# Gate and up products of the shared expert made inside the attention, their clamp made by GpSimd on the way back

## The reference

```
x = x + cross_attention(layernorm(x), ctx)      # 16 heads of 32; q, k, v and the softmax are fake-quantized
h = layernorm(x)
scores = sqrt(softplus(h @ router.T))           # 32 experts
top 4 of scores + expert_bias, their scores normalized to sum 1
x = x + sum over the 4 of share * swiglu_e(h) + swiglu_shared(h)
swiglu(h) = (silu(clip(h @ wg.T, -7, 7)) * clip(h @ wu.T, -7, 7)) @ wd.T     # inner width 256
```

## Time and profile before

| | |
|---|---|
| median of 3 runs | 1391.63 us (1389.08 to 1395.12) |
| the profiled execution's own time | 1390.22 us |
| its span, first to last instruction | 1388.2 us |
| PE busy | 1207.4 us, 87% of the span |
| DVE busy | 1104.9 us, 80% |
| ACT busy | 937.6 us, 68% |
| POOL busy | 876.1 us, 63% |
| mean granted clock of PE | 0.980 of full speed |

### The profile page before, as it was taken

The page is one execution under the profiler, slowest core; times in us unless marked ns, Lnnn a source line. Parts: engine busy times, 40 slices in busy tenths (PEclk is TensorE's granted clock), DMA queues, the critical chain, the costliest instruction groups (busy, mean ns, idle before and its releaser), DMA issues. The chain is left out here.

```text
span 1388.2 us, 29575 instructions
## 1 busy us (share of the span) xinstructions
PE 1207.4 (87%) x7490; PEld 598.3 (43%) x7587; DVE 1104.9 (80%) x2279; ACT 937.6 (68%) x1339; POOL 876.1 (63%) x897
## 2 busy tenths in 40 slices
PE   7999577888887888887888787999999999999995
PEld 3444134444444444444444343444444444444442
DVE  4567899999999999999999955674676766667663
ACT  2235499999999999999999964224555555555552
POOL 3222388998989998989898871225544454445543
PEclk9999799999999999999999989999999999999998
DMA  7564977777667676766776886646678787787442
GB/s 260 142 155 116 174 128 137 143 137 147 139 136 145 139 147 133 151 140 132 141 146 125 145 180 220 160 122 159 154 195 227 231 240 172 183 243 186 86 69 27
DMA packets 398729, 215.54 MB, mean 155 GB/s; under 512 B 357063, under 2 KB 357191, under 8 KB 398674
## 3 DMA queue, kind: packets, MB, share of 16 engines
q1 hardware_dynamic: 378338, 176.05, 53.0%
q0 software_dynamic: 20336, 38.83, 15.7%
HBM read 100.84 MB, written 37.49 MB: 100 GB/s over the span
## 5 line engine op out<-in xcount | busy, mean ns | idle before, releaser
L548 ACT ACTIVATE mem<-mem 128x2048 uint8<-128x2048 f32 x256 | 534.3, 2088 | 45.7 <-POOL mem L664 41.0
L681 POOL TENSOR_SCALAR mem<-mem 128x2048 bf16<-128x2048 uint8 x256 | 485.7, 1898 | 27.9 <-DMA mem<-mem 7.8
L462 PE MATMUL psS<-mem 128*128 128x512 bf16 x929 | 293.3, 390 | 125.5 <-DVE mem L607 56.0
L607 DVE TENSOR_SCALAR_CACHE_REDUCE mem<-psS,mem 128x1024 f32<-128x1024 f32 x256 | 327.6, 1280 | 3.4 <-PE psS L462 3.4
L591 DVE TENSOR_SCALAR_CACHE_REDUCE mem<-psS 128x1024 f32<-128x1024 f32 x256 | 312.5, 1221 | 12.7 <-PE psS L462 10.4
L1328 PE MATMUL psS<-mem 128*128 x624 | 293.9, 594 | 0.5 <-issue 0.5
L1229 POOL DMA_INDIRECT out_y<-mem x78 | 123.9, 1588 | 189.9 <-DVE mem L1405 98.6
L861 DVE TENSOR_SCALAR mem<-psS 128x512 f32<-128x512 f32 x94 | 64.9, 691 | 162.4 <-PE psS L1328 121.3
L835 PE MATMUL psS<-mem 128*128 (+1 forms) x376 | 178.4, 597 | 1.5 <-ACT mem L849 1.5
L462 PEld LDWEIGHTS psS<-mem 128*128 128x128 bf16 x1024 | 68.1, 99 | 250.3 <-DVE mem L591 155.1
L480 PEld LDWEIGHTS psAV<-mem 128*128 128x128 bf16 x4096 | 138.8, 96 | 78.9 <-POOL mem L681 23.5
(11 more groups left out here) (221 smaller groups left out, 1326.1 us busy)
## 6 DMA issues: line engine op xcount, KB each, us to landing
mem<-in_moe_w SPq DMA_DIRECT2D x64, 768.0 KB, 6.4
mem<-xn_dram SPq DMA_DIRECT2D x32, 256.0 KB, 3.0
xn_dram<-mem SPq DMA_DIRECT2D x29, 256.0 KB, 2.1
mem<-in_x SPq DMA_DIRECT2D x28, 256.0 KB, 2.9
mem<-mem SPq DMA_TRANSPOSE x292, 3.1
mem<-in_ctx_in SPq DMA_DIRECT2D x16, 256.0 KB, 3.6
out_y<-mem SPq DMA_DIRECT2D x16, 256.0 KB, 2.2
mem<-in_wkv SPq DMA_DIRECT2D x2, 1024.0 KB, 7.1
```

The costliest lines, as they stand in the source:

```text
L462: last = nc.tensor.matmul(psS[c][:, k * D:(k + 1) * D], qT[pm][:, hm, :], kT[:, hm, c * HALF + k * D:c * HALF + (k + 1) * D], start=True, ...
L548: nc.scalar.activation(p8[slot], S[slot], ACT.Exp, bias=NB[:, slot:slot + 1], scale=sq[p][:, h:h + 1], accum_out=Z[p][:, h:h + 1]).then_in ...
L607: nc.vector.tensor_scalar(S[before][:, HALF:TK], psS[1][:], 1.0, M[:, 2 * before:2 * before + 1], ALU.mult, ALU.max, accum_out=M[:, 2 * be ...
L681: nc.gpsimd.tensor_scalar(pb[slot], pT[slot].bitcast(U8).rearrange("p (j q b) -> p j b q", b=2, q=P), 1.0, 0.0, ALU.mult, ALU.add).then_in ...
```

## The change

For tiles 0 to 12 (`GATED` = 13) the gate and up products are made inside the attention. In step t (t from 3 to 15), heads 0 to 3, PE multiplies one chunk each of `xn2T`, which still holds tile t-3, by the shared gate and up weights (`gate_w`, four chunks, loaded once), into `psAV[p]` ahead of that tile's attention values. At head 4 ACT copies the result, not clamped, into `x1`; at head 6 SP stores it to a new DRAM tensor. Attention values of the step (from head 7) wait for the copy, and the next `x1` waits for the store.

After the attention SP loads the stored products into `xg` in place of `xn2`, four tiles of them before it ends. POOL clamps each in place (`clamp`), ACT takes silu from there, DVE multiplies. PE has hidden transposes and down products left for these tiles, six of them (`EARLY`) in the last 32 calls. Tiles 13 to 15 go as before, DVE clamping them out of PSUM.

The routing is cut in two: softplus, root and choice run first for tiles 0 to 13 (`TA` = 14), amid the last calls, and then for tiles 14 and 15. `soft_first`, `soft_last`, `choose_first` and `choose_last` hold the instructions that stood in a row before. The ranks need both masks. List product 0 is made behind tile 15's gate and up, the others behind its down product. The adds to the output use four buffers `y` in place of two; POOL's first gathers come after all 16 adds. `pairs` writes out the second pair of tiles too. The counts of four semaphores that the gated tiles no longer raise (`tokens_tr`, `xT_ready`, `gu_mm`, `gu_ready`) are lowered by 13 throughout.

The core of the diff:

```diff
+    GATED = TT - 3
+    EARLY = 6
+    TA = TT - 2
+    gated_dram = nc.dram_tensor("gated_dram", (T, D), F32, kind="Internal").ap()
...
+        bankE = (psS[0][:, 0:I], psS[0][:, D:D + I])
...
@@ pe_step, before the attention-value matmuls
+                if ho == 0 and gated(t):
+                    pe.wait_ge(early_out, t - 2)
...
@@ pe_step, at its end
+            if h < DC and gated(t):
+                if h == 0:
+                    if isinstance(t, int) and t == 3:
+                        pe.wait_ge(gate_w_in, 16 * DC)
+                    pe.wait_ge(x1_ready, t - 1)
+                    pe.wait_ge(router_ev, t - 2)
+                last = nc.tensor.matmul(psAV[p][:], xn2T[:, h, :], gate_w[h], start=(h == 0), stop=(h == DC - 1))
+                if h == DC - 1:
+                    last.then_inc(early_mm, 1)
...
@@ act_step
+            if h == 4 and gated(t):
+                act.wait_ge(early_mm, t - 2)
+                act.wait_ge(xn2_ready, t - 1)
+                act.wait_ge(x1_stored, 16 * (t - 1))
+                nc.scalar.activation(x1, psAV[p][:], ACT.Copy).then_inc(early_out, 1)
...
@@ sp_step
+            if isinstance(n, int) and n == H + 2:
+                for c in range(DC):
+                    sp.dma_start(gate_w[c], moe_w[E, :, c * 2 * I:(c + 1) * 2 * I]).then_inc(gate_w_in, 16)
+            if h == 6 and gated(t):
+                sp.wait_ge(early_out, t - 2)
+                apart(sp, t)
+                sp.dma_start(rows(gated_dram, t - 3), x1).then_inc(early_stored, 16)
...
@@ pairs
-            with eng.Fori(1, TT // 2 - 1) as tt:
+            for l in range(PAIR):
+                step(eng, 1, l)
+            with eng.Fori(2, TT // 2 - 1) as tt:
...
@@ act_silu (dve_hid reads gate_of(k, o) in the same way)
+        def gate_of(k, o):
+            return xg[k % MU] if isinstance(k, int) and k < GATED else gu[o]
+            if isinstance(k, int) and k < GATED:
+                act.wait_ge(early_clamped, k + 1)
+            else:
+                act.wait_ge(gu_ready, k - GATED + 1)
...
@@ pe_early
+                    pe.wait_ge(shared_in, 16 * SHARED_PIECES)
+                    for c in range(2):
+                        pe.wait_ge(half_max[c], TT * H)
+                if 2 <= l < 2 + 2 * EARLY:
+                    k = l // 2 - 1
+                    if l % 2 == 0:
+                        pe_hidden(pe, k, k % 2)
+                    else:
+                        pe_down(pe, k, k % 2, shared_weights)
+            pe.wait_ge(router_ev, TT)
+            pe.wait_ge(logits_cp, TT)
+            for k in range(EARLY, GATED):
+                pe_hidden(pe, k, k % 2)
+                if k > EARLY:
+                    pe_down(pe, k - 1, (k - 1) % 2, shared_weights)
+                if k == GATED - 4:
+                    pe_ranks(pe)
+            for k in range(GATED, SHARED):
                 o, before_o = k % 2, (k - 1) % 2
+                pe_tokens(pe, k, k % MU)
+                if k > GATED:
+                    pe_hidden(pe, k - 1, before_o)
+                pe_down(pe, k - 1, before_o, shared_weights)
+                if k == GATED:
+                    pe.wait_ge(hT_ready, GATED)
+                    pe_ends(pe)
                 pe_up(pe, k, o, shared_weights)
+            pe_list(pe, 0)
             pe_hidden(pe, SHARED - 1, (SHARED - 1) % 2)
             pe_down(pe, SHARED - 1, (SHARED - 1) % 2, shared_weights)
+            pe_experts(pe)
+            for j in range(1, TOP):
+                pe_list(pe, j)
...
@@ dve_early
+                if l == 0:
+                    dve.wait_ge(logits_cp, TA)
+                    dve.wait_ge(r_iota, 8)
+                    hidden(0)
+                    hidden(1)
+                    soft_first(most, 1)
+                    hidden(2)
+                if l == 3:
+                    soft_last(most, 1)
+                    hidden(3)
+                if l == 7:
+                    choose_first(most, range(0, TA), 1)
+                    hidden(4)
+                    choose_last(most, range(0, TA), {1: 5})
+                    then(v_.tensor_scalar(token_id, count[:, 0:TT], float(P), part[:, 0:1], ALU.mult, ALU.add))
...
@@ pool_early
-                pool_add(pool, own_rows[:, k:k + 1], y[k % 2], y_stored[k % 2])
+                pool_add(pool, own_rows[:, k:k + 1], y[k % MU], y_stored[k % MU])
+
+            def clamp(k):
+                pool.wait_ge(own_in[k % MU], 16 * (k // MU + 1))
+                nc.gpsimd.tensor_scalar(xg[k % MU][:, 0:D], xg[k % MU][:, 0:D], 7.0, -7.0,
+                                        ALU.min, ALU.max).then_inc(early_clamped, 1)
...
+                if l < MU:
+                    clamp(l)
+                if l in (5, 7, 9):
+                    clamp(MU + (l - 5) // 2)
+                if l in (6, 8):
+                    add((l - 6) // 2)
+            for k in range(2, SHARED):
+                if k + 5 < GATED:
+                    clamp(k + 5)
                 add(k)
+            pool_first(pool)
```

More of the change, by code:

```diff
@@ L953, in act_early @@
                 if l == 7:
-                    act_early_out(act, 0)
-                if l == 27:
-                    act_silu(act, 1, 1)
+                    act.wait_ge(r_soft, 1)
+                    nc.scalar.activation(first(score), first(full), ACT.Sqrt).then_inc(r_sqrt, 1)
             act.wait_ge(logits_cp, TT)
-            act.wait_ge(av_done, TT * H)
-            nc.scalar.activation(absl, logits[:], ACT.Abs).then_inc(r_abs, 1)
-            act.wait_ge(r_abs, 1)
-            nc.scalar.activation(ex, absl, ACT.Exp, scale=-1.0).then_inc(r_exp, 1)
@@ L962, in act_early @@
-            act_tokens(act, 3, 1)
-            act_hidden(act, 1, 1)
-            act.wait_ge(r_plus, 1)
-            nc.scalar.activation(lnu, u, ACT.Ln).then_inc(r_ln, 1)
-            act_early_out(act, 1)
-            act.wait_ge(r_soft, 1)
-            nc.scalar.activation(score, full, ACT.Sqrt).then_inc(r_sqrt, 1)
-            act_silu(act, 2, 0)
-            for k in range(AHEAD + 1, SHARED):
-                if k + 1 < SHARED:
-                    act_tokens(act, k + 1, (k + 1) % 2)
-                act_hidden(act, k - 1, (k - 1) % 2)
+            nc.scalar.activation(rest(absl), rest(logits), ACT.Abs).then_inc(r_abs, 1)
@@ new lines, in act_early @@
+            act.wait_ge(r_abs, 2)
+            nc.scalar.activation(rest(ex), rest(absl), ACT.Exp, scale=-1.0).then_inc(r_exp, 1)
+            act.wait_ge(r_plus, 2)
+            nc.scalar.activation(rest(lnu), rest(u), ACT.Ln).then_inc(r_ln, 1)
+            act.wait_ge(r_soft, 2)
+            nc.scalar.activation(rest(score), rest(full), ACT.Sqrt).then_inc(r_sqrt, 1)
+            for k in range(EARLY, GATED):
+                act_hidden(act, k, k % 2)
+                if k + 1 < GATED:
+                    act_silu(act, k + 1, (k + 1) % 2)
+                if k > EARLY:
+                    act_early_out(act, k - 1)
@@ new lines, in soft_last, with choose_first @@
+            def soft_last(c, turn):
+                dve.wait_ge(r_ln, turn)
+                then(v_.tensor_tensor(prod[:, c, :], prod[:, c, :], lnu[:, c, :], ALU.add))
+                v_.tensor_tensor(full[:, c, :], sel[:, c, :], prod[:, c, :], ALU.add).then_inc(r_soft, 1)
+            def choose_first(c, tiles, turn):
+                dve.wait_ge(r_sqrt, turn)
+                dve.wait_ge(r_bias, 16)
+                then(v_.tensor_tensor(sel[:, c, :], score[:, c, :],
+                                      ebias_sb[:].unsqueeze(1).to_broadcast([P, len(tiles), E]), ALU.add))
+                for t in tiles:
+                    last = v_.max(top8[:, t, :], sel[:, t, :])
+                then(last)
@@ new lines, in choose_last @@
+            def choose_last(c, tiles, between):
+                for t in tiles:
+                    last = v_.max_index(top8i[:, t, :], top8[:, t, :], sel[:, t, :])
+                then(last)
+                then(v_.tensor_copy(topf[:, c, :], top8i[:, c, 0:TOP]))
+                grid = grid_of.to_broadcast([P, len(tiles), E])
+                for j in range(TOP):
+                    then(v_.tensor_tensor(onehot[j][:, c, :], grid, topf[:, c, j:j + 1].to_broadcast([P, len(tiles), E]),
+                                          ALU.is_equal))
+                    if j >= 1:
+                        then(v_.tensor_tensor(full[:, c, :], onehot[0][:, c, :] if j == 1 else full[:, c, :],
+                                              onehot[j][:, c, :], ALU.add))
+                    if j in between:
+                        hidden(between[j])
+                v_.tensor_copy(maskb.rearrange("p (t e) -> p t e", t=TT)[:, c, :], full[:, c, :]).then_inc(r_mask, 1)
@@ L1000, in dve_early @@
+            most, last_two = slice(0, TA), slice(TA, TT)
             for l in range(PAIR):
@@ L1022, in dve_early @@
-            then(v_.tensor_scalar(token_id, count[:, 0:TT], float(P), part[:, 0:1], ALU.mult, ALU.add))
-            dve.wait_ge(r_ln, 1)
```

(29 more changed lines are left out.)

255 lines of the change are left out of this document (113 added, 142 removed).

## The result

The changed kernel takes 1399.78 us (median of 8 runs) where the kernel before, on the same chip, takes 1390.61. The ratio is 1.0064, with a 95% interval of 1.0043 to 1.0085. It is **slower by 0.64%**. The forecast was 1384.0 us, faster: the sign was wrong.

What follows compares the result with a forecast made beforehand. DVE was taken to bound attention, PE the shared and routed stages; after the change, the list chain ends the shared stage. 1390.2 - 10.2 + 1.4 + 2.6 = 1384.0 us, range 1374 to 1401.

Steps and rivals of the forecast that it cites:

- (a): After the last exponential: clamps, silu and softplus of 14 tiles delay tile 15's normalisation to 835.4, last logits to 860.9.
- (b): The two late tiles' scores: three table loads and some fifteen DVE instructions, 7.2 us, giving the mask at 868.1.
- (c): PE's three hidden transposes and down products ahead of the ranks, 6.0 us, ranks 2.3, low clock 2.3: 878.7.
- (d): DVE passes up to product 12, 6.5 us, then PE work through tile 13's up product, 8.0: gate 13 at 893.2.
- (e): Turns of gates 14 and 15, two taking 21.1 us with some low clock: gate 15 at 914.3, list at 930.6.
- The clock: PE's idle holes after attention partly lower its clock; list at 930.6, against 922.5 at full clock and 967 at half.
- no price for the clamps: POOL's 13 clamps in the shared stage, 10 us, only two on the path; port conflicts could cost up to 9.9.
- The term of attention: Gate and up pieces behind heads 0 to 3 cost 0.2 us a step at head 2, +2.6; bounds 0 to 11.2.
- The landing: Gathers behind the list land in 6.4 us beside expert loads as before; first gathered tile at 937.1, 10.2 earlier.
- the rival of dearer table switches: Each of five new ACT table exchanges on the path stalls another 1.28 us, 6.4 in all: 1390 us; chance 0.04.
- the clock keeping the list: Rival: low PE clock between waits, from ranks to last gate, delays the list to about 947: 1400 us; chance 0.17.
- The prediction's own sign: The stated test on the profile: wrong if the list is ready after 937 or before 924.

Runs made afterwards that it cites:

- loads moved: The changed kernel with the loads of the first five experts issued behind the last shared-tile load, and the store of the shares ahead of them; ratio 1.0027.
- loads moved, PE fed: The changed kernel with those expert loads moved and idle PE given products nobody reads (7 behind attention, 3 in each of two last turns); ratio 0.9986.

## Why the prediction was wrong

The account, in the prediction's own terms, of the second profile of the kernel after against the one of before (in us):

| term | forecast | measured |
|---|---|---|
| up to the first exponential | 0 | +0.1 |
| attention, first to last exponential | +2.6 | +2.9 |
| last exponential to the list | +2.7 | +16.6 |
| list to the first gathered tile on PE | -12.9 | -11.4 |
| routed stage | +1.4 | +2.5 |
| sum | -6.2 | +10.7 |

Nearly all of the error is one row, the list. Its pieces, as offsets from the last exponential (the forecast's times less 817.3):

| | forecast | after | loads moved | loads moved, PE fed |
|---|---|---|---|---|
| (a) tile 15 normalised | 18.1 | 19.0 | 19.6 | 18.2 |
| (b) mask | 50.8 | 54.1 | 54.0 | 52.6 |
| (c) ranks on VectorE | 61.4 | 66.2 | 66.2 | 61.8 |
| (d) gate 13 | 75.9 | 87.4 | 80.9 | 76.5 |
| (e) gate 15 | 97.0 | 109.3 | 104.5 | 97.9 |
| list | 113.3 | 127.3 | 121.1 | 114.7 |

**The step that failed** is piece (d), "gate 13 on DVE at 893.2". It summed the instructions of VectorE and PE and held that the tiles' data are there. From ranks to gate 13 it gave 14.5 us; 21.2 were measured, 14.7 with the experts' loads moved away. That term never asked what loads feed these tiles and what stands beside them in SyncE's queue. It is 6.7 of the 14.0 us that the list came late by; the others are 0.9 in (a), 2.4 in (b), 1.5 in (c), 0.8 in (e) and 1.7 behind it.

In the kernel before this queueing did no harm: no product of PE from 856 to 925 waits for a tile's load. There SyncE issued the ten expert loads over 36 us, in step with tiles of 5.9 us on PE; after, within 11 us. The first and the last pair in SyncE's timeline, before and then after:

```profile
842.56 0.90 SPq L1136 DMA_DIRECT2D mem<-in_moe_w  x2
878.15 1.26 SPq L1136 DMA_DIRECT2D mem<-in_moe_w  x2
...
870.03 0.90 SPq L1205 DMA_DIRECT2D mem<-in_moe_w  x2
880.60 0.98 SPq L1205 DMA_DIRECT2D mem<-in_moe_w  x2
```

The tile load issued at 884.1, behind all of them, took 19.0 us to land. With the expert loads moved the loads of the same kind took 3.8 us in the median, and 3.0 for that one. The Trainium skill (DMA: Bandwidth & Descriptors, Issuing engines are not separate DMA queues) says that transfers end up on the same 16 engines whoever issues them, and interleave there. The trace agrees: with the share at 1.04 over 40 us, clamps waited up to 5.44 us for 256 KB, and the gathers, issued by another engine, landed later beside the six expert loads (8.7 us against 3.8).

**The clock** was in the forecast, with 2.3 us in (c), 2.5 in (e) and 1.4 behind the list. Where it was tested it was sized about right: with the loads in time, feeding PE takes 3.0 us from (c) and 2.2 from (e). The sentence "few of the new holes are as long" as the 7.96 us of the earlier trace rows still misled: 7.15 us is the hole ahead of 878.27, and it stands at the head of a row of six tiles.

Loads and clock apart are worth 6.2 and 2.4 us, together 12.6: the one hides the other. With the loads moved the list stands at 121.1, still 7.8 us behind the forecast. With PE fed as well it stands at 114.7, 1.4 from it, but that is luck and no confirmation: the forecast had the low clock in it, and its own list at full clock was 105.2 (922.5). The granted clock of that run, from the last exponential to the list, is 0.86, against 0.78 without the unread products. So another 8 us or so of the chain were priced too short; the table spreads them over (a), (b), (c) and (e), and no run takes them apart.

**(e)** took the change's order as given. Its two turns came near the forecast with the low clock in, 21.9 us against 21.1; at full clock they were priced 18.6, and fed they took 21.3. With the lists ahead of the gates a turn takes 7.1. The forecast saw the turn, but not that it is an order and no need.

**Right:** the three stages, that the list and not PE would set the end, normalisation near 18, no price for the clamps, though up to 9.9 us were allowed for the port; VectorE's waits for scores (8.7 us in the same stretch as the 7.9 of the earlier trace rows). The term of attention came out at its size but in part for other reasons. In the fourteen profiles used that have the gate products, the stretch from the start of tile 2 to that of tile 15 is 1.5 to 2.7 us longer than before; in the two with the written-out pair alone, which I had priced at nothing, it is 1.4 and 1.8 longer. Set against these two, steps 7 to 13 are each 0.16 to 0.18 us longer with the gate products, near the 0.2 of the forecast, but step 14 is 1.0 us shorter, and over the whole stretch 0.4 us is left. The rest is one jump of 1.0 to 2.2 us in the step of the four weight loads, priced at nothing too, in twelve of the fourteen; its cause wasn't tested. New small waits stand where the copy is, 13.2 us in all on PE's AV products, and lie beside VectorE's work:

```profile
PE psAV L494 <- ACT mem L558: 13.2, 12, 1.2
DVE mem L623 <- PE psS L474: 8.7, 29, 0.5
```

**The landing** was priced at 6.4 and a hand-off, from rows beside expert loads; 7.9 were measured. "The same company" is a wrong reading of the earlier trace rows: before, the loads were issued 9.4 us ahead of the first gather, here 1.5. Without them PE's wait for the gather is 4.4 us shorter. Three table loads behind the last logits took 1.28 each with the next activation 1.29 or 1.30 us behind their start, as in the earlier trace rows:

```profile
869.79 1.28 ACT L1019 ACT_TABLE_LOAD   x1
871.08 0.26 ACT L1019 ACTIVATE mem<-mem 128x64 f32<-128x64 f32 x1
```

so the rival of dearer table switches fell; by the 2.66 us a switch of the Trainium skill (ScalarE: Activation LUTs, What ACT_TABLE_LOAD costs) these three would have taken 4.1 us more, and the trace doesn't agree. Of **the rivals**, the one that ends slower, with the clock keeping the list, gave 1400 us, and its sign and time are what came, by luck: its mechanism carries 2.4 us of list alone and some 5 with the loads moved, most of it already in the forecast. The late loads were in no rival. The chance of 0.19 for slower was too low for a sum that stands on one long chain with each hand-off counted at its best. The prediction's own sign came true: it was to be wrong if the list was ready after 937, and it was ready at 951.0.

## What to carry to other kernels

When work is taken from the engine that bounds a stage, list again what it had hidden or paced: ten loads that went out over 36 us went out within 11, and the small loads among them came late. Where an engine waits in its order for a product while longer work that needs nothing stands behind it, turn the order round before anything else; here this was worth 19.9 us of list, against 6.2 for the loads and 2.4 for the clock, each alone. Bulk prefetch belongs behind the small loads that the chain is waiting for.

## What was not expected of the hardware

Two groups of executions of the same code: the first exponential at 163.6 to 164.6 or at 166.7 to 168.2 us, with nothing in between, so one profile can be 4 us off for reasons that no change has; the cause is open. And a gain that hides in another: feeding PE moved the list by 6.4 us with the loads moved (5.1 of it behind the mask), by 2.4 without.
